# Second convolution of a fused vision block: batches of four images, halves and sums moved ahead, values and attention stored in its reading order

## The chip, the core and the metric

The kernel runs on one NeuronCore of a Trainium2 chip. The metric is the device time of one launch in microseconds, the lower the better. TensorE (PE) does the matrix products, VectorE (DVE), ScalarE (ACT) and GpSimd (POOL) work elementwise, SyncE (SP) issues most DMAs.

## The reference, cut to what matters

The input x is 16 images of 56 x 56 pixels with 64 channels, float32. The block adds a 3 x 3 depthwise convolution, an attention over rows and then columns whose values also pass a 5 x 5 depthwise convolution (lepe), and an MLP.

```python
x = x + _dwconv(x, pos_w, pos_b)                       # 3x3, stage "pos"
y = _layernorm(x, ln1_g, ln1_b)
q, k, v = y @ q_w + q_b, (y @ k_w + k_b) * SCALE, y @ v_w + v_b
lepe = _dwconv(v, lepe_w, lepe_b)                      # 5x5, stage "lepe"
vw  = softmax(q k^T along a row + mask_w) @ v          # 8 heads of 8
out = softmax(q k^T along a column + mask_h) @ vw
x = x + (out + lepe) @ out_w + out_b
x = x + gelu(_layernorm(x, ln2_g, ln2_b) @ fc1_w + fc1_b) @ fc2_w + fc2_b
```

## The kernel before, in words

Four stages run one after the other, each closed by a barrier of all engines: **pos** (`conv_phase` with pos true), **attention** (`attention_phase`, first all images by rows, then all images by columns), **lepe** (`conv_phase` again) and **mlp**. Between them everything goes through DRAM: `x1_d`, the normalised `xn_d`, the values `v_d`, the row attention `row_d`, the attention `att_d`, and `rt_d`, lepe plus attention transposed for the MLP.

**A convolution stage.** An image lies in a slot of `X[u]` (u is 0 or 1) with 4 x 32 partitions: partition 32 r + w holds the pixel rows whose number is r modulo 4 (RB), j = 14 of them, at column w; s tells the left from the right half of the image. A batch of up to four images is convolved at once: per group of four channels (`cg`, 16 of them) a *relay* (L1088; L1086 on ACT) gathers the channels from X into the ring `xg` of 8 slots, PE (`conv`, L1291 and L1297) multiplies with band matrices of taps, 8 fp32 products that appear as 16 matmuls, into one of four PSUM banks, and ACT copies the bank back over X (`conv_copy`, L1357). A product has 14 x 2 columns for each image of its batch: 56 for two images, 112 for four. In pos the batches have `SIZES = (2, 4, 4, 4, 2)` images, in lepe four each. Batch 0 is convolved ahead of the loop over images; in the loop `share(b, q)` gives image q of batch b its part of the 16 groups of batch b + 1. Where X[u] is used again two batches later, SP loads an image into it (`load`) once the image before is no longer read.

In pos an image then passes mean and centring (L1440, L1447 on DVE), squares, variance, root (L1264 on POOL), scaling (L1457), a bf16 half and its remainder (L1370 on ACT, L1243 on POOL), transposes (L1335) and copies (L1379 on ACT, L1468 on DVE). In lepe an image is added to its attention (`add_attention`, L1432, DVE), split into a half on ACT (`high`, L1370) and a remainder on POOL (`lo`, L1243), transposed on PE (L1335), copied by ACT into one of two `xrt` buffers (`row_copy`, L1379) and stored to `r_rows` (`store_t`, L1133). `hl` and `xrt` have two buffers each. `row_copy(n)` waits for the store of image n - 2.

The order on SP in lepe is, per image n: `load_add(n + 2)` (8 DMAs, L1119), `load(b + 2, q)` (8 DMAs, L1111, which first wait for `lo` and `high` of image n), `store_t(n - 3)`. The order on ACT is `row_copy(n - 2)`, `high(n)`, four `conv_copy`. DVE does `add_attention(n + 1)` and then four relays.

**Attention.** A chunk (v) is 14 lines of an image, a line being a pixel row in the first pass and a column in the second. TensorE's program is written out; the other engines loop over images. Two lines go side by side on partitions 0 and 64; `line_of` pairs line j with line 7 + j. `exps` (L806, ACT) writes exponentials for the product with the values; `normalise` (L892, L895, DVE) divides and writes `o_sb`. SP stores the values of a chunk with two DMAs (`store_v`, L455, to `v_d` as [image, row, column, channel]) and the result with two (`store_o`, L463), and it issues the loads and reshuffles of keys and queries (L423, L437, L469, L475, L476, L483, L484). In the column pass it loads the row attention (`load_v`, L447) instead of storing values.

Of the kernel before, what the change touches and what calls it, by code (L numbers as in the profile page):

```python
# [21 lines left out]
F32 = mybir.dt.float32  # L22
BF16 = mybir.dt.bfloat16
# [8 lines left out]
L = 56  # L32
# [213 lines left out]
def attention_phase(nc, tag, setup, x_d, v_d, row_d, att_d):  # L246
# [7 lines left out]
    with ExitStack() as ctx:  # L254
# [17 lines left out]
        o_sb = [sb(f"o_sb{u}", [128, 2, PAIRS, 32], F32) for u in range(2)]  # L272
# [25 lines left out]
        v_io = [sem(f"v_io{u}") for u in range(2)]  # L298
        o_out = [sem(f"o_out{u}") for u in range(2)]
# [129 lines left out]
        def _(sp):  # L429
# [9 lines left out]
            def load_v(i, v):  # L439
                u = v % 2  # L440
                wait(sp, vx_done, cnt(i, v, 4, -4))
                wait(sp, v_io[u], dma_count(i, v, 32) - 32)
# [7 lines left out]
            def store_v(i, v):  # L450
                u = v % 2
                wait(sp, v_sb, cnt(i, v, 1, 1))
                dst = chunk_tokens(v_d, i, v, True)
                for r in range(2):
                    sp.dma_start(dst[:, PAIRS * r:PAIRS * r + PAIRS, :],  # L455
                                 vf[u][64 * r:64 * r + L, :].rearrange("p (j c) -> p j c", c=C)).then_inc(v_io[u], 16)

            def store_o(i, v):
                u = v % 2
                wait(sp, norm_done, cnt(i, v, 1, 1))  # L460
                dst = chunk_tokens(row_d if i.rows else att_d, i, v, i.rows)
                for h in range(2):
                    sp.dma_start(dst[:, :, 32 * h:32 * h + 32],  # L463
                                 o_sb[u][64 * h:64 * h + L].rearrange("p r j c -> p (r j) c")).then_inc(o_out[u], 16)
# [80 lines left out]
            for u in range(2):  # L545
                sp.wait_ge(o_out[u], 32 * NCH)
                sp.wait_ge(v_io[u], 32 * NCH)

        @block.gpsimd
        def _(pool):  # L550
            def build_vx(i, v):
# [4 lines left out]
                else:  # L556
                    wait(pool, v_io[u], dma_count(i, v, 32))
# [74 lines left out]
        def _(pe):  # L632
# [15 lines left out]
            def project_v(i, v):  # L648
# [6 lines left out]
                for j in range(PAIRS):  # L655
                    for part, w in enumerate((w1v, w2v)):
                        for r in range(2):
                            ins = pe.matmul(pj[0][64 * r:64 * r + L, C * j:C * j + C], x[:, PAIRS * r + j, :],
# [3 lines left out]
            def line_of(v, r, j):  # L662
                return LINES * (v % 2) + PAIRS * r + j

            def scores(i, v, j):
# [19 lines left out]
                for r in range(2):  # L685
                    ln = line_of(v, r, j)
# [10 lines left out]
            def scores_t(i, v, j):  # L697
# [16 lines left out]
                for n, k in enumerate((k_hi2[w], k_lo2[w])):  # L714
                    for r in range(2):
                        ln = line_of(v, r, j)
# [66 lines left out]
        def _(act):  # L783
# [18 lines left out]
            def exps(i, v, j):  # L802
# [3 lines left out]
                act.activation(prob[t % 4][:, :, :],  # L806
                               st_ps[t % 2][:, 0:S8].rearrange("p (s q) -> p s q", q=L),
                               ACT.Exp).then_inc(exp_done, 1)
# [50 lines left out]
        def _(dve):  # L859
# [10 lines left out]
            def values(i, v):  # L870
                u = v % 2
                wait(dve, vx_done, cnt(i, v, 4, -4))
                wait(dve, v_io[u], dma_count(i, v, 32) - 32)
# [13 lines left out]
            def normalise(i, v):  # L887
# [7 lines left out]
                dve.tensor_tensor(o_sb[u][0:120].rearrange("p r j (a d) -> p (j a) r d", a=4), got[:, :, :, 0:8],  # L895
                                  sums.unsqueeze(3).to_broadcast([120, 4 * PAIRS, 2, 8]), ALU.mult).then_inc(norm_done, 1)
# [66 lines left out]
NB4 = 4  # L963
P2 = 2 * W
# [1018 lines left out]
```

## Time and profile before

| | us |
|---|---|
| median of 3 runs (2152.43 to 2163.85) | 2156.92 |
| the profiled execution | 2157.92 |
| its span, first to last instruction | 2156.1 |
| PE busy in the span | 1909.4 (89%) |
| DVE, ACT, POOL busy | 1423.9, 1248.4, 1226.2 |

The span is the time between the first and the last instruction, and 1.8 us lie around it. By the names in the trace the stages lie at 0 to 335 us (pos), 340 to 1587 (attention; its columns from about 1010), 1587 to 1835 (lepe) and 1839 to the end (mlp). An engine's busy time says how much it did, not that it set the pace; the wait shown in brackets behind an instruction says what it stood still for.

### The profile page before, as it was taken

To read this page: it belongs to the slowest core of one execution; us is meant where nothing else is said; L and a number is where in the kernel's file an instruction comes from. 1 tells how busy PE (TensorE), PEld (TensorE's weight loads), DVE (VectorE), ACT (ScalarE), POOL (GpSimd) and SP (SyncE) were. 2 spreads that over 40 slices of the span, in tenths; PEclk is the share of its full clock that TensorE was granted. 3 is DMA by queue.
4 is the path that set the end of the run, shared out by engine and by line. 5 is a ranking of instruction groups with operands and counts; after the bars stand their busy time and mean duration, and the time that the engine had idled before them with its cause. 6 is when DMAs were issued, how large, how long until landed. Compare 5 with 4: busy or idle time off the path is not lost. (4 is left out here: it accounts for less than half of the span.)

```text
span 2156.1 us, 89848 instructions
## 1 busy us (share of the span) xinstructions
PE 1909.4 (89%) x34782; PEld 1606.6 (75%) x34782; DVE 1423.9 (66%) x2254; ACT 1248.4 (58%) x2131; POOL 1226.2 (57%) x1867
## 2 busy tenths in 40 slices
PE   8977843999999999999999999999959767499998
PEld 8977742788887888877887878878849757377776
DVE  3378875677776777766776766767634433588886
ACT  3477745455555555564555555555535548388887
POOL 5367865455555554554555555555543325499997
PEclk7698865999999999999999999999979878699999
DMA  7578856778777877777777777777757787465663
GB/s 107 85 150 210 224 151 160 172 178 177 174 177 157 182 176 171 176 179 177 186 175 180 175 181 172 178 176 180 172 96 132 145 164 196 110 138 135 138 137 84
DMA packets 714019, 346.87 MB, mean 161 GB/s; under 512 B 613534, under 2 KB 672670, under 8 KB 713742
## 3 DMA queue, kind: packets, MB, share of 16 engines
q1 hardware_dynamic: 683718, 311.54, 66.0%
q0 software_dynamic: 28864, 30.98, 5.2%
q8 instruction: 237, 3.88, 0.7%
q10 hardware_dynamic: 1160, 0.13, 0.1%
q14 instruction: 40, 0.33, 0.1%
HBM read 105.42 MB, written 102.76 MB: 97 GB/s over the span
## 5 line engine op out<-in xcount | busy, mean ns | idle before, releaser
L806 ACT ACTIVATE att_prob<-att_st_ps 128x448 f32<-128x448 f32 x896 | 486.3, 543 | 448.4 <-PE att_st_ps L717 448.3
L883 DVE TENSOR_REDUCE att_mm<-att_s_ps 128x8 bf16<-128x448 f32 x896 | 556.1, 621 | 272.9 <-PE att_s_ps L687 269.2
L730 PEld LDWEIGHTS att_pv_ps<-att_vx,att_prob 128*56 128x56 f32 x14336 | 561.8, 132 | 86.3 <-ACT att_prob L806 4.7
L730 PE MATMUL att_pv_ps<-att_vx,att_prob 128*56 128x18 f32 x14336 | 514.2, 202 | 3.3 <-ACT att_prob L806 3.3
L579 POOL DMA_DIRECT2D att_mvt<-att_mneg x256 | 135.8, 535 | 557.7 <-ACT att_mneg L799 477.2
L712 PE MATMUL att_st_ps<-att_mvt,set_both 122*56 122x448 bf16 x1792 | 345.4, 357 | 20.5 <-DMA att_mvt<-att_mneg 18.9
L687 PE MATMUL att_s_ps<-att_kx,att_q_unit 120*56 120x448 bf16 x1792 | 346.8, 360 | 8.9 <-DMA att_q_unit<-att_qk_hi 4.5
L717 PE MATMUL att_st_ps<-att_qx,att_k_hi 128*56 128x448 bf16 x1792 | 344.4, 356 | 0.0
L717 PE MATMUL att_st_ps<-att_qx,att_k_lo 128*56 128x448 bf16 x1792 | 342.3, 353 | 0.0
L570 POOL DMA_DIRECT2D att_qx<-att_q_hilo x512 | 245.3, 487 | 2.0 <-issue 1.7
L793 ACT ACTIVATE att_qk_hi<-att_pj,set_bias 128x392 bf16<-128x392 f32 x256 | 150.2, 587 | 117.0 <-PE att_pj L645 116.8
L867 DVE SCALAR_TENSOR_TENSOR att_qk_lo<-att_pj,set_bias,att_qk_hi 128x392 bf16<-128x392 f32 x256 | 160.1, 626 | 78.5 <-ACT att_qk_hi L793 76.8
L1297 PEld LDWEIGHTS pos_cv_ps<-pos_xg,pos_taps 128*128 128x128 f32 x1280 | 194.9, 237 | 0.4
L1297 PE MATMUL pos_cv_ps<-pos_xg,pos_taps 128*128 128x112 f32 (+1 forms) x1280 | 193.6, 318 | 0.0
L564 POOL COPY att_vx<-att_vf 56x224 f32<-56x224 f32 x512 | 182.2, 386 | 15.9 <-DVE att_vf L875 2.2
L717 PEld LDWEIGHTS att_st_ps<-att_qx,att_k_lo 128*56 128x56 bf16 x1792 | 122.6, 108 | 51.5 <-issue 1.2
L1808 ACT ACTIVATE mlp_ht<-mlp_h_ps,mlp_b 128x392 f32<-128x392 f32 x256 | 136.6, 584 | 40.1 <-PE mlp_h_ps L1742 39.4
L645 PE MATMUL att_pj<-att_xt,set_w 128*64 128x392 bf16 x1024 | 132.9, 338 | 23.6 <-DMA att_xt<-xn_chunks 18.2
L717 PEld LDWEIGHTS att_st_ps<-att_qx,att_k_hi 128*56 128x56 bf16 x1792 | 123.0, 109 | 39.6 <-issue 1.1
L712 PEld LDWEIGHTS att_st_ps<-att_mvt,set_both 122*56 122x56 bf16 x1792 | 121.4, 107 | 38.6 <-issue 19.5
L1243 POOL TENSOR_TENSOR lepe_hl<-lepe_x,lepe_hl 128x1792 bf16<-128x1792 f32 x16 | 67.9, 4244 | 124.2 <-ACT lepe_hl L1370 123.5
L1297 PEld LDWEIGHTS lepe_cv_ps<-lepe_xg,lepe_taps 128*128 128x128 f32 x1024 | 134.8, 205 | 0.5
(209 smaller groups left out, 3321.8 us busy)
## 6 DMA issues: line engine op xcount, KB each, us to landing
att_xt<-xn_chunks SPq DMA_DIRECT2D x128, 196.0 KB, 3.5
att_k_hi<-att_qk_hi SPq DMA_DIRECT2D x128, 196.0 KB, 3.5
att_k_lo<-att_qk_lo SPq DMA_DIRECT2D x128, 196.0 KB, 3.8
att_qx<-att_q_hilo POOLq DMA_DIRECT2D x512, 49.0 KB
pos_x<-in_x_dram SPq DMA_DIRECT2D x128, 105.0 KB
lepe_x<-v_scratch SPq DMA_DIRECT2D x128, 105.0 KB, 3.2
x_scratch<-pos_x SPq DMA_DIRECT2D x128, 98.0 KB
xn_chunks<-pos_xrt SPq DMA_DIRECT2D x16, 784.0 KB, 5.2
```

Of the source, the lines that this page charges most:

```text
L564: pool.tensor_copy(dst[rows_, :, :, h, r, 0:8], src[rows_, :, :, h, :]).then_inc(vx_done, 1)
L570: pool.dma_start(head_rows(qx[w], ROW, s, 2 * KD, s * UW), head_rows(q_hilo[w], UW, s, 2 * KD, 0)).then_inc(qx_in[w], 16)
L687: ins = pe.matmul(s_ps[j % 2][64 * r:64 * r + L, 0:S8].rearrange("p (s k) -> p s k", k=L), q_unit[w][0:120, L * ln:L * ln + L], k[0:120, : ...
L712: pe.matmul(out[rs], both[0:122, rs], mvt[u][0:122, j, :, :].rearrange("p s q -> p (s q)"), start=True, stop=False)
L717: ins = pe.matmul(out[64 * r:64 * r + L].rearrange("p (s q) -> p s q", q=L), k[:, L * ln:L * ln + L], q[:, :, ln, :], start=False, stop=n ...
L730: ins = pe.matmul(pv_ps[v % 2][64 * h:64 * h + L, at:at + 18], prob[t % 4][:, 4 * h + a, :], vx[v][:, VW * j + 36 * a + 18 * h:VW * j + 36 ...
L793: act.activation(qk_hi[w][:, at:at + HALF], pj[th][:, 0:HALF], ACT.Identity, bias=bias[:, 0:1]).then_inc(qk_high, 1)
L806: act.activation(prob[t % 4][:, :, :], st_ps[t % 2][:, 0:S8].rearrange("p (s q) -> p s q", q=L), ACT.Exp).then_inc(exp_done, 1)
L867: dve.scalar_tensor_tensor(qk_lo[w][:, cols], pj[th][:, 0:HALF], bias[:, 0:1], qk_hi[w][:, cols], ALU.add, ALU.subtract).then_inc(qk_low, 1)
L883: dve.tensor_reduce(mm[v % 2][:, NH * j:NH * j + NH], s_ps[j % 2][:, 0:S8].rearrange("p (s k) -> p s k", k=L), AX.X, ALU.max).then_inc(max ...
L1297: ins = pe.matmul(cv_ps[t % 4][:, n2 * k:n2 * k + n2].rearrange("p (n j) -> p n j", j=JB), T[:, d, c, :], xg[t % RING][:, k, 0:2 * SIZES[b ...
L1808: act.activation(ht[v][:, f, HALF * h:HALF * h + HALF], h_ps[f][:, 0:HALF], ACT.Gelu, bias=b1[:, f:f + 1]).then_inc(gelu_done, 1)
```

## The change

Lepe reads `v_d` and `att_d` as [image, column w, r, j, channel], so that what a partition of X needs of an image is 14 x 64 floats in one piece; a load brings two images. The producers in attention are changed to store that way, with four DMAs instead of two for the values of a chunk. `SIZES` is dropped, and both convolutions work on four batches of four. In lepe the additions and halves of a batch are done in its first two images, `hl` has four buffers, SP stores first and then loads. Relays on DVE are a `max` of the source with itself instead of a copy.

```diff
@@ attention_phase
-        o_sb = [sb(f"o_sb{u}", [128, 2, PAIRS, 32], F32) for u in range(2)]
+        o_sb = [sb(f"o_sb{u}", [128, LINES, 32], F32) for u in range(2)]
...
             def store_v(i, v):
...
-                dst = chunk_tokens(v_d, i, v, True)
                 for r in range(2):
-                    sp.dma_start(dst[:, PAIRS * r:PAIRS * r + PAIRS, :],
-                                 vf[u][64 * r:64 * r + L, :].rearrange("p (j c) -> p j c", c=C)).then_inc(v_io[u], 16)
+                    src = vf[u][64 * r:64 * r + L, :].rearrange("p (j c) -> p j c", c=C)
+                    for e in range(2):
+                        j0 = (PAIRS * v + e) % 2
+                        at, n = (PAIRS * v + j0) // 2, (PAIRS - j0 + 1) // 2
+                        sp.dma_start(v_d[i.at, :, 2 * e + r, at:at + n, :], src[:, j0::2, :]).then_inc(v_st[u], 16)
             def store_o(i, v):
...
+                if i.rows:
+                    dst = chunk_tokens(row_d, i, v, True)
+                else:
+                    dst = att_d[i.at, LINES * v:LINES * v + LINES].rearrange("l r j c -> (r j) l c")
...
-            def line_of(v, r, j):
-                return LINES * (v % 2) + PAIRS * r + j
+            def line_of(i, v, r, j):
+                return LINES * (v % 2) + (2 * j + r if i.rows else PAIRS * r + j)
...
             def exps(i, v, j):
+                out, src = prob[t % 4][:, :, :], st_ps[t % 2][:, 0:S8].rearrange("p (s q) -> p s q", q=L)
+                if not i.rows:
+                    out = out.rearrange("p s (r j) -> p s r j", r=RB)
+                    src = src.rearrange("p s (j r) -> p s r j", r=RB)
...
             def normalise(i, v):
+                if i.rows:
+                    at = o_sb[u][0:120].rearrange("p (j r) (a d) -> p j a r d", r=2, a=4)
+                    for r in range(2):
+                        ins = dve.tensor_tensor(at[:, :, :, r, :], ...)
@@ conv_phase
-    SIZES = (2, 4, 4, 4, 2) if pos else (4, 4, 4, 4)
-    NBATCH = len(SIZES)
...
+        HL = 2 if pos else 4
+        hl = [sb(f"hl{u}", [128, NBLK, 2 * C], BF16) for u in range(HL)]
...
             if eng.engine == mybir.EngineType.Activation:
                 eng.activation(dst, src, ACT.Copy).then_inc(done, 1)
+            elif eng.engine == mybir.EngineType.DVE:
+                eng.tensor_tensor(dst, src, src, ALU.max).then_inc(done, 1)
...
+            def load_two(b, q):
+                u, n = b % 2, NB4 * b + q
+                if b >= 2:
+                    sp.wait_ge(lo_done, n - 2 * NB4 + 2)
+                    sp.wait_ge(hi_done, n - 2 * NB4 + 2)
+                for r in range(RB):
+                    m = 1 if r < 2 else 0
+                    for s in range(2):
+                        p = WB * r + 2 * (1 - s)
+                        sp.dma_start(X[u][p:p + 30, q:q + 2, s, m:m + JB, :],
+                                     src_d[n:n + 2, 26 * s:26 * s + 30, (r + 2) % RB].rearrange("b w j c -> w b j c")
+                                     ).then_inc(x_in[u], 16)
...
             def load_add(n):
                 for r in range(RB):
-                    for s in range(2):
-                        sp.dma_start(add[n % 3][WB * r + 2:WB * r + 30, s],
-                                     out_rows(add_d, n, r, s)).then_inc(add_in[n % 3], 16)
+                    sp.dma_start(add[n % 3][WB * r + 2:WB * r + 30],
+                                 add_d[n].rearrange("(s w) r j c -> r w s j c", s=2)[r]).then_inc(add_in[n % 3], 16)
...
-                elif n and n + 2 < B:
-                    load_add(n + 2)
-                if b + 2 < NBATCH:
-                    for slot in range(q, SIZES[b + 2], SIZES[b]):
-                        load(b + 2, slot)
-                if n >= LAG:
-                    store_t(n - LAG)
+                    if b + 2 < NBATCH:
+                        load(b + 2, q)
+                    if n >= LAG:
+                        store_t(n - LAG)
+                else:
+                    if n >= LAG:
+                        store_t(n - LAG)
+                    if b + 2 < NBATCH and q in (1, 2):
+                        load_two(b + 2, 2 * q - 2)
+                    if n + 3 < B:
+                        load_add(n + 3)
...
@@ scalar
-                else:
-                    high(n)
+                elif q < 2 and b + 1 == NBATCH:
+                    high(n + q)
+                    high(n + q + 1)
                 if b + 1 < NBATCH:
-                    for cg in share(b, q):
-                        conv_copy(b + 1, cg)
+                    for cg in range(4):
+                        conv_copy(b + 1, 4 * q + cg)
+                        if not pos and q < 2 and cg % 2 == 0:
+                            high(n + q + cg // 2)
@@ vector
-                elif n + 1 < B:
-                    add_attention(n + 1)
...
+                else:
+                    if q < 2:
+                        add_attention(n + q)
+                    if n + 1 < B:
+                        b1, q1 = images[n + 1]
+                        if b1 + 1 < NBATCH:
+                            for cg in range(4):
+                                relay(dve, b1 + 1, 4 * q1 + cg, relaid_dve)
+                    if q < 2:
+                        add_attention(n + q + 1)
@@ build
-    v_d = scratch("v_scratch", [B, H, W, C], F32)
+    v_d = scratch("v_scratch", [B, W, RB, JB, C], F32)
-    att_d = scratch("attention", [B, H, W, C], F32)
+    att_d = scratch("attention", [B, W, RB, JB, C], F32)
```

## Rows read from the trace of the kernel before

**Rows 1.** Busy time by stretch; at the end TensorE's granted clock, DMA share, GB/s
```profile
24.00:85.50 61.50, 61.50 (x342) 61.12 (x342) 11.01 (x23) 13.93 (x22) 11.04 (x16) 0.50 0.49 67
380.00:960.00 580.00, 568.68 (x12420) 469.14 (x12420) 420.40 (x729) 310.74 (x613) 302.27 (x676) 0.99 0.79 175
1615.00:1651.00 36.00, 35.89 (x286) 35.80 (x287) 3.25 (x5) 15.15 (x16) 14.53 (x15) 0.91 0.79 147
1695.00:1767.00 72.00, 48.46 (x384) 45.98 (x384) 23.58 (x19) 31.16 (x36) 19.16 (x8) 0.76 0.66 129
1767.00:1807.00 40.00, 38.85 (x378) 38.80 (x379) 21.56 (x20) 31.85 (x37) 17.24 (x4) 0.94 0.97 217
```

**Rows 2.** Timeline of lepe, images 5 to 7: start, duration, engine, line, idle before
```profile
1739.22 3.58 POOL L1243 TENSOR_TENSOR lepe_hl<-lepe_x,lepe_hl 128x1792 bf16<-128x1792 f32 x1 [13.65 <-ACT lepe_hl L1370]
1742.83 4.94 SPq L1111 DMA_DIRECT2D lepe_x<-v_scratch  x8
1747.82 0.44 SPq L1133 DMA_DIRECT2D r_rows<-lepe_xrt  x1
...
1752.55 2.97 ACT L1379 ACTIVATE lepe_xrt<-lepe_tr_ps 128x784 bf16<-128x784 bf16 x4 [10.27 <-DMA r_rows<-lepe_xrt]
1757.17 3.59 POOL L1243 TENSOR_TENSOR lepe_hl<-lepe_x,lepe_hl 128x1792 bf16<-128x1792 f32 x1 [14.05 <-ACT lepe_hl L1370]
```

**Rows 3.** Timeline of lepe: its start, the ends of batches, the pace of batch 2
```profile
1602.74 4.66 POOL L1223 MEMSET lepe_add<- 128x1792 f32 x3
1613.98 9.50 POOL L1088 COPY lepe_xg<-lepe_x 128x480 f32<-128x480 f32 x10 [6.58 <-DMA lepe_x<-v_scratch]
1615.43 3.59 PE L1297 MATMUL lepe_cv_ps<-lepe_xg,lepe_taps 128*128 128x112 f32 x16
...
1650.60 2.02 DVE L1432 TENSOR_TENSOR lepe_x<-lepe_x,lepe_add 128x1792 f32<-128x1792 f32 x1 [8.11 <-ACT lepe_x L1357]
...
1792.57 3.61 POOL L1243 TENSOR_TENSOR lepe_hl<-lepe_x,lepe_hl 128x1792 bf16<-128x1792 f32 x1 [2.97 <-ACT lepe_hl L1370]
...
1801.98 3.61 POOL L1243 TENSOR_TENSOR lepe_hl<-lepe_x,lepe_hl 128x1792 bf16<-128x1792 f32 x1 [5.80 <-ACT lepe_hl L1370]
...
1806.98 5.90 DVE L1432 TENSOR_TENSOR lepe_x<-lepe_x,lepe_add 128x1792 f32<-128x1792 f32 x3 [16.86 <-ACT lepe_x L1357]
1834.27 0.37 SPq L1133 DMA_DIRECT2D r_rows<-lepe_xrt  x1
```

**Rows 4.** Busy time while lepe loads its first images, and while pos does
```profile
1590.00:1614.00 24.00, 10.55 (x224) 9.94 (x224) 11.20 (x26) 9.42 (x18) 15.23 (x22) 0.64 1.03 162
4.00:20.00 16.00, 11.27 (x224) 10.59 (x224) 11.21 (x27) 8.96 (x17) 15.29 (x13) 1.00 1.00 139
```

**Rows 5.** Timeline of pos: products of batch 0, means (L1440) of images 0, 4, 5, 15
```profile
21.41 1.90 PE L1297 MATMUL pos_cv_ps<-pos_xg,pos_taps 128*128 128x56 f32 x16
...
33.27 3.53 PE L1297 MATMUL pos_cv_ps<-pos_xg,pos_taps 128*128 128x56 f32 x16
75.98 2.02 DVE L1440 TENSOR_REDUCE pos_st<-pos_x 128x28 f32<-128x1792 f32 x1 [48.25 <-ACT pos_x L1357]
145.52 2.00 DVE L1440 TENSOR_REDUCE pos_st<-pos_x 128x28 f32<-128x1792 f32 x1
160.13 2.00 DVE L1440 TENSOR_REDUCE pos_st<-pos_x 128x28 f32<-128x1792 f32 x1
...
301.70 2.01 DVE L1440 TENSOR_REDUCE pos_st<-pos_x 128x28 f32<-128x1792 f32 x1
```

**Rows 6.** By line: relays, and an ACT copy out of PSUM across 256-byte steps (L1390)
```profile
L1088 DVE COPY lepe_xg<-lepe_x x48: 690/708/4074, 1636.0 to 1787.2; 128x480 f32<-128x480 f32 x48
L1390 ACT ACTIVATE lepe_taps<-lepe_cv_ps 128x448 f32<-128x448 f32 x16 | 8.7, 572 | 3.2 <-PE lepe_cv_ps L1312 2.3
```

**Rows 7.** SP in rows: L455 (ns min/median/max); its waits 620:920 (us, times, longest)
```profile
L455 SPq DMA_DIRECT2D v_scratch<-att_vf x128: 319/601/1831, 363.8 to 954.2; - x128
...
SPq L373 <- ACT att_qk_hi L793: 9.4, 8, 3.3
```

More of the change, by code:

```diff
@@ L298, in attention_phase @@
         v_io = [sem(f"v_io{u}") for u in range(2)]
+        v_st = [sem(f"v_st{u}") for u in range(2)]
         o_out = [sem(f"o_out{u}") for u in range(2)]
@@ L963 @@
 NB4 = 4
+NBATCH = B // NB4
 P2 = 2 * W
@@ L972, in conv_phase @@
     RING = 8
-    SIZES = (2, 4, 4, 4, 2) if pos else (4, 4, 4, 4)
-    NBATCH = len(SIZES)
-    FIRST = [sum(SIZES[0:b]) for b in range(NBATCH)]
-    ZEROED = [sum(min(SIZES[a], SIZES[a + 2]) for a in range(min(b + 1, NBATCH - 2))) for b in range(NBATCH)]
-    def loaded(b):
-        return 128 * sum(SIZES[b % 2:b + 1:2])
-    def slot_uses(b, q):
-        return sum(n > q for n in SIZES[0:b + 1])
-    def share(b, q):
-        return range(16 * q // SIZES[b], 16 * (q + 1) // SIZES[b])
     with ExitStack() as ctx:
@@ L1145, in _ @@
                 sp.wait_ge(framed[b], FRAME_PARTS[b])
-                for q in range(SIZES[b]):
-                    load(b, q)
-            sp.wait_ge(framed_rest, 1)
+                for q in range(0, NB4, 1 if pos else 2):
+                    (load if pos else load_two)(b, q)
             if not pos:
@@ L1248, in ahead @@
                 if n < len(images) and images[n][0] + 1 < NBATCH:
-                    for cg in share(*images[n])[1::2]:
-                        relay(pool, images[n][0] + 1, cg, relaid)
+                    for cg in (1, 3):
+                        relay(pool, images[n][0] + 1, 4 * images[n][1] + cg, relaid)
             for cg in range(16):
@@ L1397, in ahead @@
                 if n < len(images) and images[n][0] + 1 < NBATCH:
-                    for cg in share(*images[n])[0::2]:
-                        relay(act, images[n][0] + 1, cg, relaid_act)
+                    for cg in (0, 2):
+                        relay(act, images[n][0] + 1, 4 * images[n][1] + cg, relaid_act)
             if pos:
@@ L1503, in _ @@
             if not pos:
-                for cg in share(0, 0):
+                for cg in range(4):
                     relay(dve, 1, cg, relaid_dve)
-                add_attention(0)
             for n, (b, q) in enumerate(images):
@@ L1518, in _ @@
                         col_copy(n - 2, range(2, G))
-                elif n + 1 < B:
-                    add_attention(n + 1)
-                    b1, q1 = images[n + 1]
-                    if b1 + 1 < NBATCH:
-                        for cg in share(b1, q1):
-                            relay(dve, b1 + 1, cg, relaid_dve)
+                else:
+                    if q < 2:
[3 more added lines that the diff above has]
+                        if b1 + 1 < NBATCH:
+                            for cg in range(4):
+                                relay(dve, b1 + 1, 4 * q1 + cg, relaid_dve)
+                    if q < 2:
+                        add_attention(n + q + 1)
             if pos:
```

110 lines of the change are left out of this document (51 added, 59 removed).

## The prediction

> **What bounds the kernel now.** I read the busy time by stretch first [rows 1]. In attention PE is busy 568.68 of 580 us at a granted clock of 0.99, so that stage goes at PE's pace. Lepe does not: from 1695 to 1767 PE is busy 48.46 of 72 us, no engine more, and the DMA share is 0.66. Four images took 72 us there, four of the next batch 40 us (1767 to 1807). That is the place to look at.
>
> The timeline of the slow four [rows 2] shows a ring of waits. POOL's remainder (L1243) starts at 1739.22 and, one image later, at 1757.17: 17.95 us, of which it stood 14.05 waiting for ACT's half. ACT had stood 10.27 us ahead of its row copies (L1379) for the store of an older image to land. SP issued such a store (L1133, 1747.82) only behind eight loads (L1111), and those had waited for POOL's remainder. So: remainder, loads, store, landing, row copy, half, next remainder. Nothing in it is long; it is serial. Where SP has nothing to load (batch 2) the same remainder starts every 9.41 us, from 1792.57 to 1801.98 [rows 3].
>
> **The change part by part, lepe.** *The ring.* Storing first means that a store waits for row copies alone, and four `hl` buffers let the halves run up to four images ahead of the transposes. I take the pace of batch 2 for all twelve images that have convolutions beside them. They lasted from 1650.60 to 1806.98 [rows 3], 156.4 us; 12 x 9.41 is 112.9: **-43.5 us**. What is late next is PE: four groups at 1.96 us each (1.93 in the timeline, as of L1297 at full clock) and 28 transposes are some 9.4 us an image. Against it: in the first two images of a batch ACT has row copies 2.97, two halves of 1.72 and four copies of 0.95, 10.2 us, 0.8 more than PE, six to eight images long, partly covered by the four banks: **+3**.
>
> *The border between batches.* Both additions of images 2 and 3 come an image or two earlier, so X is free earlier and the next batch's relays find it loaded. PE's waits at borders are inside the 156.4 us and need no second term.
>
> *Transfers.* An image moves 8 x 105, 8 x 98 and 784 KB, 2.47 MB, wherever a load runs beside it, which is 8 images. At 9.41 us that asks for 262 GB/s; batch 2 already has a DMA share of 0.97 at 217 GB/s with 256-byte pieces in its additions [rows 1]. Pieces of 3584 bytes cannot be priced in this stage. If they gave nothing over 217, an image would take 11.4 us, 8 x 2.0 is +16; if they are free, 0. I take **+4**, nearer the second, because in attention, where most bytes go in long pieces, 175 GB/s needs a share of only 0.79 [rows 1].
>
> *Start.* Loads of the first four images land at 1613.98, 23.5 us after their issue, at 162 GB/s with the share at 1.03 [rows 4]. At 220 they would take 16 us and be there at 1606. POOL then sets the start: it clears the addition buffers until 1607.4 [rows 3] and relays from there. So 1613.98 becomes 1607.4: **-7**; nothing if long pieces are no faster.
>
> *The end.* The last four images take 27.3 us, from 1806.98 to 1834.27 [rows 3]. ACT has six row copies and four halves there, 24.8 us: **-2**.
>
> *Relays as max.* A plain relay takes 708 ns, and up to 4074 when POOL reads beside it [rows 6]. DVE's addition of 1792 elements takes 2.02 us, so 480 elements of a two-input form come to some 0.67 us; strided they could be up to twice that. DVE and POOL seem to exclude each other on such forms, so their sum counts: 3.6 for the remainder, 2.02 for the addition, four relays of 0.67 to 1.3: 8.3 to 10.8 us an image against PE's 9.4. I take 0, with +12 as the far end (12 images at 1.0 more). The Trainium skill speaks against the edit here: "SBUF — State Buffer", section "Who interferes with whom", says that a DVE instruction with two SBUF inputs contends with a GpSimd instruction that reads SBUF, so the new form would not set POOL free. The 4074 ns of the plain copy agrees that the lock exists for the old form as well; by the rule the sum does not gain from this edit, by a reading in which max never blocks it would gain nothing either, as PE is late next. Lepe in all: -43.5 + 3 + 4 - 7 - 2 = **-45.5**.
>
> **Pos.** The batches of 2, 4, 4, 4, 2 become four of 4. *Batch 0 loads twice as much.* 3.44 MB and some 0.4 MB of parameters beside it, at the 139 GB/s of 4 to 20 us [rows 4], take 28 us; clearing X takes 1.6 us longer, so loading begins at 5.4 and ends at 33.4, the first product starts at 34.4 in place of 21.41 [rows 5]: +13. *Batch 0's products.* There are 16 groups of 16 matmuls, whatever the width. With 56 columns a group takes 3.5 us [rows 5], and the granted clock is 0.50 from 24.0 to 85.5 although PE is busy all of that time [rows 1]. Lepe runs the same groups with 112 columns, back to back like these, at 0.91 [rows 1]; 16 of them last from 1615.43 to about 1649.6, 34.2 us. I take that in place of 54: -19.8. The first mean (75.98) comes at 69.3: **-6.7**. *Images 0 to 4.* They lasted 145.52 - 75.98 = 69.5 us, because two images carry all 16 groups of batch 1 and the third waits for them. Spread over four images, they cost the first two some 11 us each and the rest 14.6 (from 145.52 to 160.13), with transfers at their limit: 54 us: **-15.5**. *Images 4 to 15.* 156.2 us for eleven images, helped by a small last batch; at 14.6 they make 160.6, and one border more: **+6**. Pos in all: **-16**.
>
> **Attention.** Sixty-four chunks of values go out with four DMAs instead of two. SP's waits in 300 us of the row pass come to 9.4 us [rows 7], 0.6 us per pair of chunks (18.7 us): it is almost full. Two issues of L455 and their address arithmetic take from 0.9 us; a pair of chunks gets four more, 1.8 to 3.5 us. Unabsorbed, that is +1.2 to +2.9 a pair, 38 to 93 us over 32 pairs. But the same transfer is issued in 319 ns and in 1831 [rows 7]: much of an issue is waiting for room behind earlier transfers, and the bytes stay as they are. So I take **+3**, with 0 and 93 as ends. Normalising in two halves adds some 0.15 us on DVE per chunk, covered by DVE's 160 idle us of 580 [rows 1]. Exponentials in permuted order read PSUM across 16-byte steps; L1390 reads 448 elements across 256-byte steps in 572 ns [rows 6], so I price it at 0; at worst ACT, busy 54% of the pass, hides it too. The order of stored attention becomes that in which row attention is stored already: 0. Mlp is not touched: 0.
>
> **Sum.** -45.5 - 16 + 3 = -58.5 from the profiled execution's 2157.9 is 2099.4. The median of the runs is 1.0 us lower, within their scatter, so I say 2100.
>
> **The rivals.** *A: the clock stays low.* If width was not the cause, batch 0 of pos takes 16 x 3.6 us, 24 us more: 2124. For it: PE was busy all the time the clock was down, so idleness did not lower it. Against it: it fell 3 us after the 56-column products began and rose when 112 columns followed, and lepe shows 0.91. [...] *B: SP is partly unabsorbed*, 1.2 us a pair: 2138. *C: long pieces are no faster* than 162 GB/s: 2.47 MB take 15.2 us, 8 x 5.8 more, and no earlier start: some 2150. For it: DMA share 0.97. Against it: attention. *D, slower: SP becomes the bound of the row pass.* Every added issue costs in full, 2.9 us a pair, +93 instead of +3: 2190. It decides the sign from 2.2 us a pair beyond SP's slack; PE would then show waits for queries and keys, which it hardly has now. *E: the change undoes one thing with another* or does not reach its aim: about 2157.
>
> **How the numbers follow.** Forecast 0.60, A 0.12, B 0.10, C 0.08, D 0.06, E 0.04. A measurement of this kernel tells 0.5%, 11 us, from no change. Faster takes forecast, A, B and most of C: 0.89; same 0.05; slower 0.06. The range reaches down to a pos and lepe without my three allowances and with a full clock from the first group (2078), and up to B and near C (2146).
>
> **What would show it.** Right: remainders of lepe 9.4 to 10.3 us apart in every batch, no row copy waiting for a store, lepe about 200 us long; first mean of pos near 69 us with the clock up during batch 0; attention as long as before. Wrong: clock 0.50 during batch 0 of pos; PE waiting for DMAs of L423, L475 or L483 in the row pass; remainders of the first batches slower than 11 us with the DMA share at 1.

## The result and the profile after

The changed kernel takes 2174.99 us, median of 12 runs (2163.86 to 2190.26), against 2158.03 us, median of 12 runs of the kernel before (2145.23 to 2168.66). The ratio is 1.0079 with an interval of 1.0051 to 1.0106: slower, by some 17 us, where 58 us less were predicted. The profiled execution took 2171.25 us.

Stage by stage (first to last instruction of a stage, before and after): pos ends at 332.8 and at 313.3, **-19.5**. Attention lasts 1241.3 and 1276.5, **+35.2**, all of it in the row pass (the stores of the column pass, 566.1 us before, take 560.4). Lepe lasts 247.4 and 243.9, **-3.5**. Mlp 312.8 and 313.6. So one term came as forecast, one cost twelve times what it was priced at, and the largest gain did not appear: against the forecast attention is 32 us too long and lepe 42.

The busy time by stretch of the kernel after (PE, PEld, DVE, ACT, POOL busy, granted clock, DMA share, GB/s), to be read beside [rows 1]:

```profile
24.00:85.50 61.50, 48.23 (x431) 47.53 (x431) 14.99 (x26) 23.95 (x25) 24.59 (x22) 0.86 0.73 111
380.00:960.00 580.00, 555.52 (x11939) 451.83 (x11937) 404.81 (x759) 293.84 (x582) 285.19 (x638) 0.98 0.74 164
```

In pos the granted clock over 24 to 85.5 us is 0.86 where it was 0.50, and PE has 48.23 us of work where it had 61.50. The products of batch 0, now of 112 columns, begin at 34.93; from 44 us on the clock is 1.00, the level of 2.4 GHz, where it was 0.50, the level of 1.2 GHz, until about 85 us. In the row pass PE, which was the bound with 568.68 of 580, is busy 13 us less of the same time: it now waits, and something else sets the pace. Over the whole pass (363.8 to 954.2 before, 343.8 to 977.2 after) PE stands idle for 40.1 us in place of 16.0, and the same matmuls keep it busy for 593.3 us in place of 574.4, at a clock of 0.96 in place of 0.98. So 24 of the 43 us are time in which PE stands, and the other 19 are the same work done more slowly.

Lines, and what they waited for: the means (channel averages) of pos, with the times of the first and the last; values stored by SP in the row pass; SP's waits in 620 to 920 us (the only row of that answer); PE's largest wait in 380 to 960; lepe's products, relays and remainders.

```profile
L1455 DVE TENSOR_REDUCE pos_st<-pos_x x16: 2001/2007/2022, 70.4 to 282.2; 128x28 f32<-128x1792 f32 x16
...
L461 SPq DMA_DIRECT2D v_scratch<-att_vf x256: 319/394/1820, 343.8 to 977.2; - x128
...
SPq L374 <- ACT att_qk_hi L801: 1.1, 1, 1.1
...
PE att_pj L653 <- DMA att_xt<-xn_chunks: 21.2, 18, 2.0
...
L1310 PE MATMUL lepe_cv_ps<-lepe_xg,lepe_taps x1024: 258/275/423, 1628.1 to 1818.9; 128*128 128x112 f32 x171
...
L1088 DVE TENSOR_TENSOR lepe_xg<-lepe_x x48: 1224/1263/4620, 1647.6 to 1793.4; 128x480 f32<-128x480 f32 x48
...
L1257 POOL TENSOR_TENSOR lepe_hl<-lepe_x,lepe_hl x16: 3573/3596/18960, 1666.0 to 1838.3; 128x1792 bf16<-128x1792 f32 x16
```

Two lengths are used as yardsticks below. The value stores run from 343.8 to 977.2, **633.4 us**, against 590.4 before [rows 7]: the row pass. Lepe's products run from 1628.1 to 1818.9, **190.8 us**; before:

```profile
L1297 PE MATMUL lepe_cv_ps<-lepe_xg,lepe_taps x1024: 258/275/422, 1615.4 to 1805.7; 128*128 128x112 f32 x171
```

That is 190.3 us. PE's 21.2 us for its tokens (`xn_chunks`, loaded by SP) were 2.1 before. SP's wait of 9.4 us in 300 has shrunk to 1.1: SP has no slack left. A relay takes 1263 ns at the median where it took 708 [rows 6], and a remainder once took 18.96 us where its usual length is 3.6. The timeline of the other long one, of 17.97 us, at a border between two batches of lepe:

```profile
1697.68 3.49 SPq L1109 DMA_DIRECT2D lepe_x<-v_scratch  x8
...
1708.00 4.71 DVE L1088 TENSOR_TENSOR lepe_xg<-lepe_x 128x480 f32<-128x480 f32 x4 [13.82 <-DMA lepe_x<-v_scratch]
1712.63 2.01 DVE L1447 TENSOR_TENSOR lepe_x<-lepe_x,lepe_add 128x1792 f32<-128x1792 f32 x1
1714.57 2.97 ACT L1391 ACTIVATE lepe_xrt<-lepe_tr_ps 128x784 bf16<-128x784 bf16 x4 [9.74 <-DMA r_rows<-lepe_xrt]
1714.57 4.85 DVE L1088 TENSOR_TENSOR lepe_xg<-lepe_x 128x480 f32<-128x480 f32 x4
...
1719.32 3.97 DVE L1447 TENSOR_TENSOR lepe_x<-lepe_x,lepe_add 128x1792 f32<-128x1792 f32 x2
1719.96 17.97 POOL L1257 TENSOR_TENSOR lepe_hl<-lepe_x,lepe_hl 128x1792 bf16<-128x1792 f32 x1 [21.99 <-ACT lepe_hl L1382]
1723.19 4.82 DVE L1088 TENSOR_TENSOR lepe_xg<-lepe_x 128x480 f32<-128x480 f32 x4
...
1727.90 2.03 DVE L1447 TENSOR_TENSOR lepe_x<-lepe_x,lepe_add 128x1792 f32<-128x1792 f32 x1
1729.84 4.66 DVE L1088 TENSOR_TENSOR lepe_xg<-lepe_x 128x480 f32<-128x480 f32 x4
...
1737.99 3.10 PE L1348 MATMUL lepe_tr_ps<-lepe_ident_b,lepe_hl 128*128 128x128 bf16 x28 [9.63 <-POOL lepe_hl L1257]
...
1738.22 3.57 POOL L1257 TENSOR_TENSOR lepe_hl<-lepe_x,lepe_hl 128x1792 bf16<-128x1792 f32 x1
...
1741.82 4.70 SPq L1109 DMA_DIRECT2D lepe_x<-v_scratch  x8
...
1768.17 4.71 DVE L1088 TENSOR_TENSOR lepe_xg<-lepe_x 128x480 f32<-128x480 f32 x4 [33.68 <-DMA lepe_x<-v_scratch]
```

The remainder starts at 1719.96, and VectorE works without a gap until 1734.5 (additions, four relays, an addition, four relays). Take those 14.5 us off and 3.4 are left, about the remainder's usual length. So it seems to have stood until VectorE paused, and PE waited 9.63 us for it. The loads of two images wait for the remainders of both: they went out at 1741.82, behind the next remainder, and those of the other two images at 1749.56. The relays of the next batch then stood 33.68 us for them. That is how one late remainder becomes a long border.

### The profile page after: what moved, and what is told of

Read it like the earlier page. It is cut to its first block and busy times, and to the rows that moved or that the text cites. A ratio compares the mean times of both kernels' runs of the same rounds, so it can differ in the third digit from the quotient of the medians.

```text
span 2169.1 us, 89542 instructions
## 1 busy us (share of the span) xinstructions
PE 1862.2 (86%) x34510; PEld 1547.4 (71%) x34510; DVE 1435.9 (66%) x2318; ACT 1244.2 (57%) x2107; POOL 1250.8 (58%) x1858
## 5 line engine op out<-in xcount | busy, mean ns | idle before, releaser
L1257 POOL TENSOR_TENSOR lepe_hl<-lepe_x,lepe_hl 128x1792 bf16<-128x1792 f32 x16 | 93.8, 5880 | 99.1 <-ACT lepe_hl L1382 99.1
L1310 PEld LDWEIGHTS pos_cv_ps<-pos_xg,pos_taps 128*128 128x128 f32 x1024 | 139.3, 211 | 0.6
L1310 PE MATMUL pos_cv_ps<-pos_xg,pos_taps 128*128 128x112 f32 x1024 | 137.4, 293 | 0.0
L695 PEld LDWEIGHTS att_s_ps<-att_kx,att_q_unit 120*56 120x56 bf16 x1792 | 121.5, 109 | 18.9 <-issue 10.3
```

The lines of the kernel that those rows point to most:

```text
L695: ins = pe.matmul(s_ps[j % 2][64 * r:64 * r + L, 0:S8].rearrange("p (s k) -> p s k", k=L), q_unit[w][0:120, L * ln:L * ln + L], k[0:120, : ...
L1310: ins = pe.matmul(cv_ps[t % 4][:, P2 * k:P2 * k + P2].rearrange("p (n j) -> p n j", j=JB), T[:, d, c, :], xg[t % RING][:, k, :, d:d + JB], ...
```

## The experiments

Each is given with its edit to the kernel before, to the kernel after or to an earlier run. Ratios are to the kernel before. The diffs are cut; semaphores and counts that change along with them are left out. Times are medians of 4 to 10 executions; the length of a stage comes from the one that was profiled, and is less sure than it looks. Attention is the same program in runs 3, 5, 8 and 9, and the row pass lasted 603.3, 606.6, 595.0 and 594.7 us; in the change and run 4 it lasted 633.4 and 638.3. Lepe is the same program in runs 4 and 5 and lasted 222.2 and 213.2; untouched, it lasted 241 to 249 us in the kernel before and runs 1, 2 and 6, so the change's -3.5 us is no difference.

**1. Pos alone.** On the kernel before:

```diff
-    SIZES = (2, 4, 4, 4, 2) if pos else (4, 4, 4, 4)
+    SIZES = (4, 4, 4, 4)
```

> The kernel before with four batches of four images in the first convolution too, nothing else. Theory: the 19.5 us by which the first convolution is shorter in the changed kernel (last instruction 332.8 to 313.3) come from this alone, by the higher clock in batch 0 and the even spread of batch 1: first mean near 70 us, total 2157 - 20 = 2138. Rival: the shorter stage owes something to another edit of the change; then less than 10 us are gained here (2148 or more).

2132.35 us, 0.9865 (0.9801 to 0.9929); pos ends at 312.1. The same stretch of that run and its means:

```profile
24.00:85.50 61.50, 47.55 (x431) 46.85 (x431) 15.08 (x23) 24.64 (x26) 25.36 (x22) 0.87 0.77 110
...
L1440 DVE TENSOR_REDUCE pos_st<-pos_x x16: 2000/2008/2020, 69.7 to 281.0; 128x28 f32<-128x1792 f32 x16
```

This part of the change is worth some 20 us by the trace and does it by itself (26 by the medians, whose interval is wide). The first mean comes at 69.7, the clock is up.

**2. Four stores a chunk alone**, to the same places as before (4 and 3 lines a DMA in place of 7):

```diff
-                    sp.dma_start(dst[:, PAIRS * r:PAIRS * r + PAIRS, :], ...).then_inc(v_io[u], 16)
+                    for e in range(2):
+                        at, n = 4 * e, 4 - e
+                        sp.dma_start(dst[:, PAIRS * r + at:PAIRS * r + at + n, :], src[:, at:at + n, :]).then_inc(v_st[u], 16)
```

> The kernel before with the values of a chunk stored by four DMAs (4 and 3 lines) instead of two, to the same places, nothing else. Theory: SP's queue is full in the row pass, so the two more issues per chunk lengthen it from 37.6 to about 40 us per image, PE waits for loads of xt, total 2157 + 40 = 2197. Rival: the longer row pass comes from the new pairing of lines, the halves of normalise or the new places in DRAM; then this kernel stays within 10 us of 2157.

2211.21 us, 1.0221 (1.0146 to 1.0295). Its value stores, and PE's largest wait in 380 to 960 us:

```profile
L461 SPq DMA_DIRECT2D v_scratch<-att_vf x256: 319/362/1937, 365.9 to 1014.2; - x128
...
PE att_pj L650 <- DMA att_xt<-xn_chunks: 38.0, 35, 2.5
```

648.3 us in place of 590.4, SP without a wait from 620 to 920. The same bytes to the same places, only in twice as many DMAs, cost 57.9 us here, 1.8 us a pair of chunks. So the issues alone cost as much as the change did and more: its layout and its halves of the normalisation need not have cost anything.

**3. SP relieved.** On the kernel after, the DMAs of the eight heads' keys, of which SP issued six and POOL two:

```diff
-        K_SP, K_POOL = range(0, 6), range(6, NH)
+        K_SP, K_POOL = range(0, 4), range(4, NH)
```

> The changed kernel with the key rows of four heads filled from SP's queue and of four from POOL's (six and two before), so SP issues two DMAs of 0.56 us less per pair of chunks, POOL two more. Theory: with SP relieved by 1.2 us a pair of chunks the row pass goes back from 40.2 to about 37.8 us per image, total 2175 - 38 = 2137. Rival: SP's queue is not what holds the row pass; then it stays at 40 us per image, or POOL's two more issues make it longer.

2136.9 us, 0.9883 (0.9821 to 0.9946).

```profile
L461 SPq DMA_DIRECT2D v_scratch<-att_vf x256: 319/351/1656, 338.6 to 941.9; - x128
...
PE att_pj L653 <- DMA att_xt<-xn_chunks: 6.1, 5, 1.8
```

603.3 us: of the 43.0 us that the row pass had gained in length, 30.1 are gone, and PE's wait for its tokens fell from 21.2 to 6.1. By the four traces with this split, 27 to 39 us are gone and 4 to 16 remain. The column pass, in which POOL issues two more as well, took 571.7 us in place of 560.4. Lepe is as long as in the change (its products 190.5 us).

**4. Relays as copies again.** On the kernel after:

```diff
-            elif eng.engine == mybir.EngineType.DVE:
-                eng.tensor_tensor(dst, src, src, ALU.max).then_inc(done, 1)
```

> The changed kernel with the relays on DVE as plain copies again, nothing else. Theory: a max of two SBUF inputs takes 1.24 us instead of 0.71 and, back to back, keeps POOL's remainder out (18 and 19 us for those of images 4 and 8 instead of 3.6); the late remainders make the loads late. With copies those remainders take under 8 us and the second convolution falls from 244 to about 215 us, total 2175 - 30 = 2145. Rival: transfers bound the borders (1.72 MB per load of two images at 212 GB/s); then the stage stays above 235 us and the total above 2165.

2153.71 us, 0.9973 (0.9938 to 1.0007).

```profile
L1308 PE MATMUL lepe_cv_ps<-lepe_xg,lepe_taps x1024: 258/275/421, 1639.3 to 1807.3; 128*128 128x112 f32 x171
...
L1088 DVE COPY lepe_xg<-lepe_x x48: 685/707/4310, 1659.7 to 1798.3; 128x480 f32<-128x480 f32 x48
...
1678.19 14.33 POOL L1255 TENSOR_TENSOR lepe_hl<-lepe_x,lepe_hl 128x1792 bf16<-128x1792 f32 x1 [19.48 <-ACT lepe_hl L1380]
```

Products over 168.0 us, 22.8 less. The stage was 222.2 us, not the 215 expected, and one remainder still took 14.33 us, beside additions and plain relays; under 8 was expected. Runs 3 and 4 together win back most of what was missing. The first loss is the price of the new layout, which needs four stores a chunk; the second comes from an edit at the side of it.

**5. Both repairs together.**

> The kernel after with both repairs: VectorE's relays as plain copies, and the keys' DMAs split 4 on SP and 4 on POOL. Theory (two separate losses, in two separate stages: SP's issues in the row pass, the max relays in the convolution): they add, 2175 - 21 - 38 = 2116 us, row pass 615 us, convolution 222 us. Rival (one loss seen twice, the end of one stage moved into the next): one repair gives nearly all, 2135 us or more.

2117.56 us (2105.81 to 2120.74), **0.9793** (0.9747 to 0.9839): they add. Lepe lasted 213.2 us, its products 159.9:

```profile
L1308 PE MATMUL lepe_cv_ps<-lepe_xg,lepe_taps x1024: 258/275/422, 1605.8 to 1765.7; 128*128 128x112 f32 x171
```

In 620 to 920 us SP still had no wait.

**6. Keys' split on the kernel before**, the edit of 3.

> The kernel before with the keys' DMAs split 4 on SP and 4 on POOL instead of 6 and 2, nothing else. SP waited only 9.4 us of 300 in its row pass. Theory (before, SP was just below the bound): no change within 0.5%, 2150 to 2165 us. Rival (SP bounded the row pass already, and what the change did was only more of it): row pass shorter by 15 us or more, 2143 us or less. Rival (POOL, with more to issue, is late for the units): 2170 us or more.

2159.88 us, 1.0003 (0.9983 to 1.0023). SP's waits in 620 to 920 and the value stores:

```profile
SPq L373 <- ACT att_qk_hi L793: 31.1, 16, 3.7
...
L455 SPq DMA_DIRECT2D v_scratch<-att_vf x128: 319/617/1894, 368.3 to 958.5; - x128
```

SP waited 31.1 us for 9.4, and the row pass was as long as before (590.2). So before SP was just below the bound, and freeing it was worth nothing by itself. (The profiled execution was the slowest of the ten, 2177.30 us; its column pass took 579.0 us.)

**7. The ring alone.** On the kernel before, stores first and four buffers for the halves; relays, layout, additions as before:

```diff
+        HL = 2 if pos else 4
-        hl = [sb(f"hl{u}", ...) for u in range(2)]
+        hl = [sb(f"hl{u}", ...) for u in range(HL)]
...
-                elif n and n + 2 < B:
-                    load_add(n + 2)
+                else:
+                    if n >= LAG:
+                        store_t(n - LAG)
+                    if n and n + 2 < B:
+                        load_add(n + 2)
```

> The kernel before with two parts of the change alone, in the second convolution: SP issues the store of three images ago before it waits for the load, and the halves have four buffers. Old layout of the values, old relays, adds and halves in the old order. The prediction's ring term in full: convolution 247.4 - 43.5 = 204 us, 2115 us in all. Rival (stores and halves were one of several waits of equal length, the loads and the adds come next): 225 to 240 us, 2135 to 2150 us in all. Rival (the order of the stores did nothing): 247 us.

2142.96 us, 0.9937 (0.9911 to 0.9964); lepe 225.3 us, between the theories: 22.1 us less, not 43.5. The products, and ACT's row copies:

```profile
L1301 PE MATMUL lepe_cv_ps<-lepe_xg,lepe_taps x1024: 258/275/421, 1621.5 to 1790.6; 128*128 128x112 f32 x171
...
1691.49 2.97 ACT L1383 ACTIVATE lepe_xrt<-lepe_tr_ps 128x784 bf16<-128x784 bf16 x4 [0.42 <-DMA r_rows<-lepe_xrt]
1712.58 3.00 ACT L1383 ACTIVATE lepe_xrt<-lepe_tr_ps 128x784 bf16<-128x784 bf16 x4
1722.02 3.01 ACT L1383 ACTIVATE lepe_xrt<-lepe_tr_ps 128x784 bf16<-128x784 bf16 x4
1731.41 3.00 ACT L1383 ACTIVATE lepe_xrt<-lepe_tr_ps 128x784 bf16<-128x784 bf16 x4
```

Within a batch the row copies come every 9.4 us and wait for no store but for 0.42 us at its end: the ring is gone. But at the border 21.1 us lie between two of them (1691.49 to 1712.58), and 21.3 at the next (1742.11 to 1763.40). Each is 11.7 to 11.9 us over the pace, 23.6 together, about what is missing of the 43.5.

**8. Loads of one image.** On run 5:

```diff
-                for q in range(0, NB4, 1 if pos else 2):
-                    (load if pos else load_two)(b, q)
+                for q in range(NB4):
+                    load(b, q)
...
-                    if b + 2 < NBATCH and q in (1, 2):
-                        load_two(b + 2, 2 * q - 2)
                     if n + 3 < B:
                         load_add(n + 3)
+                    if b + 2 < NBATCH:
+                        load(b + 2, q)
```

> As the run with both repairs, but the second convolution loads its values one image a load again (8 DMAs an image of one 1792-byte piece a pixel row each, issued as soon as that image's halves are done, behind the loads of what is added). Theory (the border now waits for loads that are issued late, because one load waits for the halves of two images and holds the stores behind it on SP): the convolution goes from 222 to 205-212 us, VectorE's waits for loads from 45 us to under 20, ScalarE's for stores to under 10. Rival (the transfers themselves set the border, 0.9 MB a half batch at some 210 GB/s): 222 us within 3. Rival (SP's 32 more issues a batch are late): 225 us or more.

2123.05 us, 0.9829 (0.9796 to 0.9862), with lepe 233.8 us: 20.6 more than run 5, where less was expected. (The piece a load moves is 3584 bytes in run 5 and in this one, and half a batch is 1.72 MB; the text above misstates both.) VectorE's wait, and the stretch before it ends:

```profile
DVE lepe_xg L1088 <- DMA lepe_x<-v_scratch: 61.1, 2, 32.6
...
1644.00:1678.00 34.00, 22.13 (x220) 21.92 (x220) 1.38 (x2) 16.33 (x20) 12.32 (x8) 0.86 0.90 218
```

From 1644 to 1678 the DMA share is 0.90 at 218 GB/s. The last load is issued by 1665.5 and lands at 1677.7. Issuing early did not make the bytes arrive early: this theory falls. The number is that of the last rival (225 us or more, SP's issues are late), and SP issued nearly without a gap from 1644.57 to 1665.88, so it is not excluded. Nor is the order of the loads (the additions' now go ahead of each image's), nor a remainder of 14.34 us that fell in this trace; they were not separated. Against run 4, the same lepe as run 5, it is 11.6 us.

**9. Additions ahead of relays.** On run 5, in VectorE's loop:

```diff
                     if q < 2:
                         add_attention(n + q)
+                        add_attention(n + q + 1)
...
-                    if q < 2:
-                        add_attention(n + q + 1)
```

> The run with both repairs, and in the second convolution VectorE adds images 0 and 1 of a batch before the relays of image 1, and 2 and 3 before those of image 2 (in the change each second add stands behind four relays, and the relays of the ring wait for TensorE). Theory (at a border the relays wait 14 to 18 us for the last load, which SP issues only when the halves of image 3 are done, and these only after an add that waits behind relays): that load goes out up to 9 us earlier, the convolution falls from 213 to 196-205 us, 2100 to 2109 us in all. Rival (the loads' own transfers, some 10 us a pair of images, and their fight with the loads of the attention's output set the border): 210 to 214 us. Rival (early adds make the relays late and TensorE waits for them): 216 us or more.

2105.94 us (2103.39 to 2118.23), **0.9759** (0.9722 to 0.9795). But lepe lasted 215.2 us, as in run 5. The remainders of images 2 to 4:

```profile
1644.07 8.58 POOL L1255 TENSOR_TENSOR lepe_hl<-lepe_x,lepe_hl 128x1792 bf16<-128x1792 f32 x1 [4.84 <-ACT lepe_hl L1380]
1652.94 3.59 POOL L1255 TENSOR_TENSOR lepe_hl<-lepe_x,lepe_hl 128x1792 bf16<-128x1792 f32 x1
1678.92 3.72 POOL L1255 TENSOR_TENSOR lepe_hl<-lepe_x,lepe_hl 128x1792 bf16<-128x1792 f32 x1 [22.07 <-ACT lepe_hl L1380]
...
L461 SPq DMA_DIRECT2D v_scratch<-att_vf x256: 319/376/1764, 339.5 to 934.2; - x128
```

The additions came early, yet the last load of the border still went out only at 1656.55, 89.1 us after the stage's first instruction, as in run 5 (1668.80, 88.8 us), behind image 3's remainder (1652.94), which had stood behind image 2's, 8.58 us long beside eight relays. The addition was not what made it late. The 12 us between this run and run 5 lie in the row pass (594.7 against 606.6 us), which this edit does not touch; in run 8, with the same row pass, it is 595.0. So runs 5 and 9 are one result, 2106 to 2118 us, and the gain of run 9 is not shown.

**10. Keys 2 and 6.** On run 9, `K_SP, K_POOL = range(0, 2), range(2, NH)`.

> As the run with the early adds, but with 2 of the 8 keys' DMAs on SP and 6 on POOL. With 4 and 4 SP had still no wait that the trace shows in 300 us of the row pass, and TensorE still waited 13.5 us for the tokens. Theory (SP is still just at the bound): the row pass goes from 618 to some 605 us, 10 to 14 us less in all than the run beside it. Rival (POOL, which has more to issue and the wider work, becomes late): the same or slower than the run beside it, by up to 15 us.

2131.73 us, 0.9869 (0.985 to 0.9888), 26 us slower than run 9. The row pass gained 4 us (590.9), and the column pass lost 26: its stores of attention run from 985.7 to 1581.8, 596.1 us, against 570.1 in run 9. PE's wait there, in 1000 to 1570 us:

```profile
PE att_st_ps L720 <- DMA att_mvt<-att_mneg: 33.9, 27, 3.3
```

In run 9 it was 12.4 us. These DMAs are POOL's. SP now waited 22.4 us of 300 in the row pass. So SP was hardly the bound there any more, and POOL's queue became late in the column pass: the rival holds, and of these splits four and four is the best.

**11. Max relays on the kernel before.** The two lines of 4 added there.

> The kernel before with VectorE's 48 relays of the second convolution (and none else) as max of a value with itself, as the change has them. Theory (a max relay takes 1.24 us for 0.71, but a relay stands in no chain that sets the end of an image there; it cost 21 us in the change because relays and adds then filled VectorE at the borders, next to the halves on GpSimd): convolution 247 to 252 us, ratio 1.000 to 1.003. Rival (each relay is on the path, 0.53 us each): 48 of them, 25 us more, 2183 us. Rival (GpSimd's halves are stretched wherever a max runs beside them): they take over 6 us each in place of 4.2, 10 us or more in all.

2183.33 us, 1.0101 (1.008 to 1.0121). My theory (no cost there) is refuted; the 22 us agree with 48 times 0.53 us, and remainders were stretched as well, to 12.7, 14.4 and 21.0 us. What each of the two rivals is worth is not separated.

```profile
L1299 PE MATMUL lepe_cv_ps<-lepe_xg,lepe_taps x1024: 258/275/422, 1619.1 to 1831.4; 128*128 128x112 f32 x171
...
L1245 POOL TENSOR_TENSOR lepe_hl<-lepe_x,lepe_hl x16: 3578/3837/21029, 1657.4 to 1852.7; 128x1792 bf16<-128x1792 f32 x16
```

**12. One input, same duration.** On the kernel before, a relay as one copy that writes its values twice, the second time to a place nobody reads (`xg2`, the ring with room for both):

```diff
+            elif eng.engine == mybir.EngineType.DVE:
+                twice = [128, 2, 4, 2 * NB4 * (JB + 1)]
+                eng.tensor_copy(xg2[t % RING][:, :, :, :, :].rearrange("p r c n j -> p r c (n j)"),
+                                src.unsqueeze(1).to_broadcast(twice)).then_inc(done, 1)
```

> The kernel before with VectorE's 48 relays of the second convolution as one copy each that writes its 480 values twice (the second time beside the first, read by nobody): one input, and a duration about that of the max relay or above. Theory (a max relay costs what it lasts, wherever it stands): as the run with max relays on the kernel before, convolution some 268 us, 2180 us in all; halves on GpSimd at 3.6 to 7 us. Rival (a max relay costs because it reads two inputs and holds back the halves that run beside it on GpSimd, which took 12.7, 14.4 and 21.0 us in that run): the doubled copy stretches no half over 8 us, convolution 247 to 253 us, ratio 1.000 to 1.004. In between: both.

2185.51 us, 1.0095 (1.0065 to 1.0125).

```profile
L1302 PE MATMUL lepe_cv_ps<-lepe_xg,lepe_taps x1024: 258/275/422, 1618.9 to 1832.1; 128*128 128x112 f32 x171
...
L1090 DVE COPY lepe_xg<-lepe_x x48: 1233/1270/4621, 1639.5 to 1806.3; 128x960 f32<-128x960 f32 x48
...
1789.81 21.23 POOL L1248 TENSOR_TENSOR lepe_hl<-lepe_x,lepe_hl 128x1792 bf16<-128x1792 f32 x1 [13.46 <-ACT lepe_hl L1375]
```

1.27 us a relay, products over 213.2 us (212.3 in run 11), and remainders of 14.6 and 21.2 us where run 11 had 14.4 and 21.0. A copy with one input does what the max did; only the remainder of 12.7 us in run 11 has no match here (3.8). The expected time came, the expected 3.6 to 7 us for the remainders did not. So it is not the two inputs but the length of a relay. The kernel before shows the same place at 0.71 us a relay:

```profile
1701.15 7.26 POOL L1243 TENSOR_TENSOR lepe_hl<-lepe_x,lepe_hl 128x1792 bf16<-128x1792 f32 x1 [15.73 <-ACT lepe_hl L1370]
...
1703.00 1.95 DVE L1088 COPY lepe_xg<-lepe_x 128x480 f32<-128x480 f32 x3
1705.28 3.65 DVE L1088 COPY lepe_xg<-lepe_x 128x480 f32<-128x480 f32 x1 [0.33 <-PE lepe_cv_ps L1297]
```

There VectorE had to wait 0.33 us for PE, the remainder got in, and it was VectorE that stood, with a relay of 3.65 us. At 1.25 us a relay VectorE did not catch up with PE in these stretches and left GpSimd no gap. Short relays make this rarer and do not rule it out, as the 14.33 us of run 4 show.

## Why the prediction was wrong, point by point

**Attention, "So I take +3, with 0 and 93 as ends": the step that failed most**, +35.2 measured. The prediction had the right row (SP full but for 9.4 us in 300), and the right price of what stays unabsorbed (+1.2 to +2.9 us a pair of chunks). It then argued the price away: much of an issue is waiting for room, and the bytes stay. Run 2 shows the bytes unchanged and 1.8 us a pair lost; run 3 takes issues off SP and regains 30 us. The change itself cost 43.0 / 32 = 1.3 us a pair, close to what rival B set; for attention alone B was the right case, and rival D (SP becomes the bound of the row pass) the right mechanism at less than half its price. D's sign was that PE waits for queries and keys; it waited for tokens (L437 before), which stand in the same queue. Why split stores in the old layout (run 2) cost 15 us more than the change's was not tried.

**"Relays as max. I take 0, with +12 as the far end": the second**, 22 to 31 us measured on the products (run 4 against the change 22.8; run 5 against run 3, 30.6; run 11 on the kernel before 22.0), 19 to 22 by the medians. The estimate of 0.67 us, "strided up to twice that", was taken at its low end; 1.26 us was the other. By the far end's own sum DVE and POOL came to 10.8 us an image against PE's 9.4; that is 1.4 us an image, 17 in all, and was priced at 1.0 and 12. What the sum missed is that the loss is not even: at a border VectorE has a backlog, and one remainder then waits out all of it. The Trainium skill, "SBUF — State Buffer", section "Who interferes with whom", names copies in a two-port mode beside two-input forms among those that contend with GpSimd. Which mode a relay's copy runs in no trace shows; run 12's copy of 960 elements held a remainder as long as the max did.

**"The ring: -43.5": right mechanism, half the size.** Run 7 shows it: 9.4 us an image inside a batch and hardly a row copy waiting for a store, as predicted. (In the changed kernel they waited at the borders, once 9.74 us.) The mis-sized part is the sentence "PE's waits at borders are inside the 156.4 us and need no second term". They were inside the 156.4 before, but 12 x 9.41 leaves them out after. The two borders of run 7 cost 23.6 us over the pace. "X is free earlier and the next batch's relays find it loaded" did not happen: after the change the relays stood 13.82 and 33.68 us for loads at the two borders, 47.5 in all. They stood 10.4 in the kernel before, 15.9 in run 7, and even with plain relays 45.5 in run 4 and 32.1 in run 5, where a load brings two images and waits for both. What the pair loads cost or give alone was not run. With plain relays lepe is 213.2 us (run 5) or 222.2 (run 4), against 201.9 by my sum, which has the relays at 0: 25 to 34 of the 45.5 us.

**Start of lepe, "-7".** Measured -3: the first product comes 25.5 us after the stage's first instruction in place of 28.6. The first loads were issued at 1606.27, and POOL's first relay started at 1626.64, 20.4 us later; the sum had 16. In that stretch 198 GB/s moved at a share of 0.93, where pieces of 256 bytes had 162 at 1.03 [rows 4] and I took 220. So rival C did not occur: the long pieces are faster, but not by what I took.

**Pos, "-16": right**, -19.5 and -20.7 (run 1). First mean predicted 69.3, measured 70.4; images 0 to 4 lasted 54.5 us (54 predicted); the clock is 0.86 against 0.50, so rival A did not occur. Images 4 to 15 took 157.3 us where 160.6 were predicted and 156.2 had been: the +6 was too much.

**The range** reached to "B and near C", 2146. It gave no place to several faults at once: the issues and the relays, each named and priced and taken near its cheap end, and the borders of the ring, priced at nothing.

## What to carry to other kernels

Where a queue's own waits show it nearly full, charge every added issue at its whole price, and only then look for slack; or move issues to another queue in the same edit (here two of six DMAs moved to another queue turned 0.8% slower into 1.2% faster). Before writing a copy in another form, measure its duration: where two engines hold each other off and one works in bursts, double the length can take away the gap in which the other gets in. When a ring of waits is opened, sum the borders between batches apart from the pace within one. And try the parts alone: on the kernel before, the batches of pos won 26 us (run 1) and the ring 15 (run 7) by the medians. If the two add, which was not run, they come to some 2117 us, as long as the whole change with both repairs. Beyond the 3 us at the start of lepe, nothing that the new layout gives is shown.

## What the runs showed of the hardware

VectorE's max of 480 strided float32 elements with itself lasts 1263 ns at the median, a plain copy of the same 707, a copy of them to two places 1270. A GpSimd subtraction of 1792 elements that began while VectorE worked without a gap lasted 17.97 us for its usual 3.6, until VectorE paused, whether VectorE's work between its additions was max (14.4 and 21.0 us, run 11), the long copy (14.6 and 21.2, run 12) or, once, the plain one (14.33, run 4). In the last row of run 12 VectorE's last relay ended at 1807.60, and the subtraction 3.4 us later. I had expected a hold for the length of one instruction. And loads in pieces of 3584 bytes ran at 218 GB/s with a DMA share of 0.90 (run 8) and at 198 with 0.93 (start of lepe in the changed kernel), where 256-byte pieces had 162 at 1.03 [rows 4] and a mix with them 217 at 0.97 [rows 1]: little for pieces fourteen times as long.
